# Attention and a mixture of experts on one core: the batches of the attention stage written out, two orders changed

## The chip, the core and the metric

The kernel runs on one core of a Trainium2 chip. The core has a matrix engine (TensorE, PE in the profile, with its weight loads as PEld), three engines for element-wise work (VectorE DVE, ScalarE ACT, GpSimd POOL) and a queue engine that issues most transfers (SyncE, SP). Each engine takes its own list of instructions in order; engines meet at semaphores. The metric is the device time of one execution in microseconds. Before the change it is 4362.92 us (median of 3 runs, 4358.69 to 4367.35).

## The reference

One transformer block in float32 over x of shape 8 x 1024 x 512. Cut to what matters:

```
q, k, v = heads(x @ Wq.T + bq), heads(x @ Wk.T + bk), heads(x @ Wv.T + bv)   # 16 heads of 32
q_lr, k_lr = q @ Wq_lsr, k @ Wk_lsr                                            # per head, rank 32
attn = softmax(causal(q_lr @ k_lr.T / sqrt(32)))
x = layernorm(x + (attn @ v) @ Wo.T + bo)
# experts: 16 of them, each takes the 512 tokens with the largest logit for it
xn = x / rms(x) * norm_weight;  logits = xn @ router.T + bias
y_e = gelu(xn[idx_e] @ fc1_e.T + b1) @ fc2_e.T + b2,   weighted by softmax(logits), summed per token
x = layernorm(x + weighted sum / sum of weights)
```

## The kernel before, in words

The program runs five stages one after the other: folding the weights, attention, selection of tokens, experts, last normalisation. The diff touches the attention stage, `build_attention`, and the lists that order it.

Attention goes batch by batch, eight batches (NB = 8) of 1024 tokens. Per batch there are four slots, one for each group of four heads (`plan_slot`), and then an output phase (`plan_tail`). The lists that these functions return hold items such as ("scores", g, k, h) or ("out", t), and every engine walks through the same list and does its part of each item. So the list sets the order on TensorE, ScalarE, VectorE and GpSimd together. SyncE has its own order, written out in its `run`.

In a slot TensorE makes scores of key blocks (L682), ScalarE takes exponentials into `probs` (L796), GpSimd masks the diagonal blocks (L541), and TensorE multiplies probabilities with values and with ones (L701). Between these stand, for the groups to come, projections of q and k (L670, "proj") and products whose row maxima VectorE takes (L637, L640, L845). Before the next group's operands can be used, SyncE copies strips of q and k into them (`strips`, L435 and L436: 24 transfers) and loads the next weights (L422).

The output phase has eight token tiles, t = 0 to 7. "out" is the product with Wo (L670 from `y_cols`); behind it come, on the other engines, the residual added on VectorE (L878), the statistics (L880), two square roots on ScalarE (L766, L768), and the two normalised forms x1 and xn (L887, L896), both stored by SyncE (L478, L480). "turn" transposes xn on TensorE (L656), ScalarE copies the result into xnT (L772). "logit" is the product with the router for four tiles (L664), copied by L777 and stored by L473. "v" is the value product of the next batch (L670 from `wv_parts`), copied by ScalarE (L728). "invert" is the reciprocal of softmax sums (L869), which belongs to the last group. All products of out, v, turn and logit go through a ring of three banks, `shared_banks`, in the order of the list; a bank is free when its reader is done: for "out" that is the statistics instruction L880.

The residual of tile 0 is loaded before the last group's strips are issued, that of tile 1 after them (L441, in `run` of SyncE).

`probs` has four buffers. x1 is buffer 0, xn buffer 1, xnT buffers 2 and 3. `slot_of(k, pair)` says which buffer the exponentials of key block k use. At the first exponential of a batch ScalarE waits until all stores of x1 and xn are done (L787 to L791).

`each_batch` runs the first seven batches as a loop on the engines, with the batch number in a register, and writes the last batch out behind it. The last batch leaves out the work for a batch to come: no "v" items, and fewer projections and maxima. `lead` is the work before the first batch.

Of the kernel before, what the change touches and what calls it, by code (L numbers as in the profile page):

```python
# [21 lines left out]
GROUPS = HEADS // HG  # L22
T = 1024
TT = T // P
# [7 lines left out]
QT = HALF // P  # L32
# [154 lines left out]
PROB_BUFS = 4  # L187
DEN_PIECES = 4
TURN_LAG = 2
# [43 lines left out]
def plan_tail():  # L233

    order = []
    for t in range(TT + TURN_LAG):
        if t < TT:
            order.append(("out", t))
            if t == 0:
                order += [("invert", GROUPS - 1, 1, i) for i in range(2)]  # L240
            order.append(("v", t))
            if t == 0:
                order += [("invert", GROUPS - 1, 1, i) for i in range(2, DEN_PIECES)]
        if t >= TURN_LAG:
            order.append(("turn", t - TURN_LAG))
            if (t - TURN_LAG) % QT == QT - 1:
                order.append(("logit", (t - TURN_LAG) // QT))
    return order


def plan_lead():
# [23 lines left out]
def build_attention(nc, w, x_dram, xT_dram, x1_dram, table, logits_dram, scratch, keep, NB):  # L275
    with ExitStack() as ctx:
# [11 lines left out]
        v = sb("v_rows", [P, TT, D])  # L288
# [60 lines left out]

        def slot_of(k, pair):  # L350

            return (2 * k + pair) % PROB_BUFS

        assert PROB_BUFS == 4 and (2 * NE) % PROB_BUFS == 0

# [24 lines left out]
        def scope(b, lead=False):  # L380

            if lead:
                return lead_in, lead_turns, [0] * RING
            off = [lead_used[k] + b * batch_used[k] for k in range(RING)]
            if isinstance(b, int) and b == NB - 1:
                return last, last_turns, off
            return batch, batch_turns, off

        def seen_by(b, item, lead=False):

            if lead:
                return lead_seen[item]
            return (last_seen if isinstance(b, int) and b == NB - 1 else batch_seen)[item]

        def await_parts(eng, passed, b, g, lead=False):

# [4 lines left out]

        def each_batch(eng, run):

            if NB > 1:
                with eng.Fori(0, NB - 1) as b:
                    run(b)
            run(NB - 1)

        block = ctx.enter_context(nc.Block())

# [1 line left out]
        def _(sp):  # L412
# [28 lines left out]
                sp.dma_start(xres[:, t % 2], x_dram[bass.ds(b * T + t * P, P), :]).then_inc(res_in[t % 2], 16)  # L441

            def run(b):
                more = not (isinstance(b, int) and b == NB - 1)
                for slot in range(GROUPS - AHEAD):
                    strips(b, slot)
                    if more or slot + 1 < GROUPS - AHEAD:
                        load_w((slot + AHEAD + 1) % GROUPS)
                if more:
                    load_x(b + 1, b * GROUPS + GROUPS)  # L450
                    strips(b, GROUPS - 2)
                    load_w(1)
                load_residual(b, 0)
                if more:
                    strips(b, GROUPS - 1)
                    load_w(2)
                for t in range(1, TT + TURN_LAG):

                    if t < TT:
                        load_residual(b, t)  # L460
                    if t >= TURN_LAG:
                        store(b, t - TURN_LAG)
                        if t - TURN_LAG == QT:
                            store_logits(b, 0)
                store_logits(b, 1)
# [36 lines left out]
        def _(pool):  # L502
# [48 lines left out]

            def run(b):
                order, _, _ = scope(b)
                more = not (isinstance(b, int) and b == NB - 1)
                for item in order:
                    if item[0] == "invert" and item[3] == DEN_PIECES - 1:
                        normalise(b, item[1], item[2])
# [155 lines left out]
        def _(act):  # L713
# [70 lines left out]
            def exps(b, g, k, h):  # L784
                c0 = steps[k][2]
                s = (b * GROUPS + g) * NE + k
                act.wait_ge(st_full, HG * s + h + 1)  # L787
                if g == 0 and k == 0 and h == 0:

                    for r in range(2):  # L790
                        act.wait_ge(x1_out[r], 16 * (TT // 2) * b)  # L791
                        act.wait_ge(xn_out[r], 16 * (TT // 2) * b)
# [898 lines left out]
```

## Time and profile before

| what | value |
|---|---|
| median of 3 runs | 4362.92 us |
| the profiled execution: time, span | 4363.62 us, 4361.9 us |
| mean granted TensorE clock | 0.914 |
| TensorE busy | 3794.3 us, 87% of the span |
| VectorE, ScalarE, GpSimd busy | 52%, 34%, 16% |

A row of the timeline gives start and length in us, engine, source line, operation, output and input tiles, shapes and how often; a bracket at its end is the time that the engine was idle before, and what released it ("issue": nothing that the profile shows). Starts count from the beginning of the span. Attention ends at about 2570 us of it, experts take most of the rest. The granted clock is given as a share of 2.4 GHz: 1.00, or 0.50 for 1.2 GHz.

### The profile page before, as it was taken

The page shows a single profiled execution, that of the slowest core. Times are in us where ns is not written, and L with a number is a line of the kernel's source. Part 1 is how long each engine was busy: PE and PEld are TensorE (multiplying, and loading weights), DVE is VectorE, ACT ScalarE, POOL GpSimd, SP SyncE. Part 2 cuts the span into 40 slices and gives each one's busy share as a digit, 9 for nine tenths or more (in the row PEclk, how much of TensorE's full clock was granted, in tenths as well). Part 3 has the DMA queues.
Part 4 walks back from the last instruction along what each step waited for, and adds up shares of the span by engine and source line. Part 5 has one row for each costly group of instructions (what it writes and reads, how often), then busy time and mean ns, then how long its engine had stood idle before and what let it go on. Part 6 is the DMA issues. An engine that isn't in the chain of part 4 may idle for free. (4 is left out here: it accounts for less than half of the span.)

```text
span 4361.9 us, 64361 instructions
## 1 busy us (share of the span) xinstructions
PE 3794.3 (87%) x21481; PEld 2590.9 (59%) x21481; DVE 2257.6 (52%) x3990; ACT 1471.7 (34%) x2754; POOL 686.1 (16%) x859
## 2 busy tenths in 40 slices
PE   5898999998998998989989951799999999999990
PEld 3555555555555555555555420788888888888880
DVE  3565555554664654655655547544444444444444
ACT  1342432442442433433434410333333333333324
POOL 2121121121121121211211110011111111021100
PEclk8899999998999999999999975599999999999995
DMA  4224233133133322331342120233334433344328
GB/s 151 63 77 117 58 86 105 46 100 96 42 98 96 80 75 82 98 91 55 91 113 64 35 64 0 88 119 119 118 104 128 128 119 119 114 122 124 119 68 317
DMA packets 187436, 424.18 MB, mean 97 GB/s; under 512 B 39776, under 2 KB 42848, under 8 KB 178400
## 3 DMA queue, kind: packets, MB, share of 16 engines
q1 hardware_dynamic: 167408, 367.98, 28.0%
q0 software_dynamic: 14336, 34.09, 4.3%
q10 hardware_dynamic: 5376, 17.83, 1.0%
q8 instruction: 207, 3.39, 0.3%
q14 instruction: 109, 0.89, 0.1%
HBM read 245.70 MB, written 72.38 MB: 73 GB/s over the span
## 5 line engine op out<-in xcount | busy, mean ns | idle before, releaser
L845 DVE TENSOR_REDUCE max_slots<-shared_banks 128x1 f32<-128x512 f32 (+3 forms) x1536 | 790.0, 550 | 501.4 <-PE shared_banks L640 378.7
L796 ACT ACTIVATE probs<-scores_t 128x512 f32<-128x512 f32 (+3 forms) x1536 | 677.8, 494 | 789.7 <-PE scores_t L682 733.9
L1514 PE MATMUL m_ps_h<-m_tokens_t,m_w_parts 128*128 128x512 f32 x3072 | 743.4, 391 | 15.2 <-issue 13.6
L1514 PE MATMUL m_ps_y<-m_w_parts,m_hidden_parts 128*128 128x512 f32 x3072 | 736.5, 389 | 0.3
L1514 PEld LDWEIGHTS m_ps_h<-m_tokens_t,m_w_parts 128*128 128x128 f32 x3072 | 575.1, 188 | 138.5 <-issue 20.6
L1514 PEld LDWEIGHTS m_ps_y<-m_w_parts,m_hidden_parts 128*128 128x128 f32 x3072 | 575.9, 188 | 123.1 <-issue 3.7
L637 PE MATMUL shared_banks<-k_operands,q_operands 96*128 96x512 f32 (+3 forms) x1536 | 540.1, 403 | 89.6 <-DMA k_operands<-natural 79.1
L682 PE MATMUL scores_t<-q_operands,k_operands 128*128 128x512 f32 (+3 forms) x1536 | 543.3, 404 | 51.0 <-ACT probs L796 22.6
L637 PEld LDWEIGHTS shared_banks<-k_operands,q_operands 96*128 96x128 f32 x1536 | 314.0, 207 | 273.1 <-issue 134.2
L1421 ACT ACTIVATE m_hidden<-m_ps_h,m_b 128x512 f32<-128x512 f32 x256 | 176.6, 690 | 834.2 <-PE m_ps_h L1514 821.0
L541 POOL TENSOR_SCALAR_AFFINE_SELECT probs<-probs 128x256 f32<-128x256 f32 x512 | 208.3, 408 | 1431.3 <-ACT probs L796 1431.1
L1479 DVE CAST m_hidden_parts<-m_hidden 128x512 fp32r<-128x512 f32 x256 | 110.7, 432 | 599.2 <-ACT m_hidden L1421 599.0
L670 PE MATMUL shared_banks<-x_parts,wqk_group 128*128 128x512 f32 x1536 | 385.4, 403 | 32.9 <-DVE x_parts L901 18.3
L682 PEld LDWEIGHTS scores_t<-q_operands,k_operands 128*128 128x128 f32 x1536 | 287.4, 203 | 188.1 <-issue 109.0
L701 PE MATMUL y_bank<-probs,v_rows 128*32 128x512 f32 (+3 forms) x3072 | 348.8, 528 | 1.5 <-POOL probs L541 1.5
L670 PEld LDWEIGHTS shared_banks<-x_parts,wqk_group 128*128 128x128 f32 x1536 | 289.9, 194 | 96.7 <-issue 19.1
L701 PE MATMUL den_bank<-probs,ones_f 128*32 128x512 f32 (+3 forms) x3072 | 326.8, 498 | 0.0
L1379 POOL DMA_INDIRECT scratch_x<-m_out,m_idx x64 | 114.0, 1781 | 1160.6 <-DVE m_out L1498 1146.0
L670 PE MATMUL shared_banks<-wv_parts,x_parts 128*128 128x512 f32 x768 | 227.9, 450 | 67.4 <-DVE ln_stats L880 67.1
L640 PE MATMUL shared_banks<-mask_q_rows,ident_bf 128*128 128x128 bf16 x1024 | 246.2, 243 | 0.0
L670 PE MATMUL shared_banks<-wo_cols,y_cols 128*128 128x512 f32 x512 | 236.1, 605 | 4.2 <-DVE ln_stats L880 4.2
L670 PEld LDWEIGHTS shared_banks<-wv_parts,x_parts 128*128 128x128 f32 x768 | 156.4, 205 | 130.9 <-DVE ln_stats L880 72.8
(202 smaller groups left out, 3205.3 us busy)
## 6 DMA issues: line engine op xcount, KB each, us to landing
m_w_raw<-in_w1T SPq DMA_DIRECT2D x64, 1024.0 KB, 5.1
m_w_raw<-in_w2T SPq DMA_DIRECT2D x64, 1024.0 KB, 7.4
q_operands<-natural SPq DMA_DIRECT2D x384, 128.0 KB, 2.5
k_operands<-natural SPq DMA_DIRECT2D x384, 128.0 KB, 2.5
wqk_group<-scratch_wqk SPq DMA_DIRECT2D x32, 1024.0 KB, 5.2
natural<-in_xT SPq DMA_DIRECT2D x8, 2048.0 KB, 8.7
x_residual<-in_x SPq DMA_DIRECT2D x64, 256.0 KB, 2.8
scratch_x<-probs SPq DMA_DIRECT2D x64, 256.0 KB, 2.1
```

The lines of the kernel that those rows point to most:

```text
L541: pool.affine_select(out=block, in_=block, compare_op=ALU.is_ge, fill=0.0, base=0, pattern=[[0, 2], [1, P]], channel_multiplier=-1).then_i ...
L637: mm = pe.matmul(out[:, 0:n], q_ops[0:MAX_STRIP, buf, h, it * P:(it + 1) * P], k_ops[0:MAX_STRIP, buf, h, k0:k0 + n], start=True, stop=not ...
L640: mm = pe.matmul(out[:, n - P:n], identb[:], mask_q[:], start=False, stop=True)
L670: mm = pe.matmul(out, a, c, start=(n == 0), stop=(n == len(pairs) - 1))
L682: pe.matmul(st[:, (HG * k + h) % SCORE_BANKS, c0:HALF], k_ops[:, buf, h, j * P:(j + 1) * P], q_ops[:, buf, h, hh * HALF + c0:(hh + 1) * HA ...
L701: mm = pe.matmul(bank[h * DH:(h + 1) * DH, c0:HALF], rows(h, j), probs[:, slot_of(k, h // 2), h % 2, c0:HALF], start=(j == 0), stop=(j == ...
L796: act.activation(probs[:, slot_of(k, h // 2), h % 2, c0:HALF], st[:, (HG * k + h) % SCORE_BANKS, c0:HALF], ACT.Exp, scale=SCALE).then_inc( ...
L845: dve.tensor_reduce(mx[:, h, slot:slot + 1], src[:, 0:n], AX.X, ALU.max).then_inc(bank_free[bank], 1)
L1379: pool.indirect_dma_start(out=x1_dram[:, :], out_offset=bass.IndirectOffsetOnAxis(ap=idx[:, r, j:j + 1], axis=0), in_=out[:, j, :], in_off ...
L1421: act.activation(h[:, f % 2, :], ps_h[:, f % 2, 0:CAP], ACT.Gelu, bias=b1[:, r, f:f + 1]).then_inc(gelu_done, 1)
L1479: dve.tensor_copy(hs[:, f % 2, HI, :], h[:, f % 2, :]).then_inc(h_hi, 1)
L1514: mm = pe.matmul(bank, a, b, start=(first and n == 0), stop=(final and n == len(pairs) - 1))
```

## The change

Three things. `each_batch` writes all eight batches out, so no engine has a loop or a batch number in a register here. `slot_of` is shifted by two buffers: the first key block of a batch uses buffers 2 and 3, and ScalarE's wait for the stores of x1 and xn moves from the first key block to the second (and is dropped for the first batch). `plan_tail` orders a tile as out, turn of two tiles before, values of the tile before; all four reciprocals follow the first out; the last turns, the last values and the second logits come at the end. The other lines take away a test that only a loop needs.

```diff
--- before.py
+++ after.py
@@ -233,19 +233,17 @@
 def plan_tail():
 
     order = []
-    for t in range(TT + TURN_LAG):
-        if t < TT:
-            order.append(("out", t))
-            if t == 0:
-                order += [("invert", GROUPS - 1, 1, i) for i in range(2)]
-            order.append(("v", t))
-            if t == 0:
-                order += [("invert", GROUPS - 1, 1, i) for i in range(2, DEN_PIECES)]
+    for t in range(TT):
+        order.append(("out", t))
+        if t == 0:
+            order += [("invert", GROUPS - 1, 1, i) for i in range(DEN_PIECES)]
         if t >= TURN_LAG:
             order.append(("turn", t - TURN_LAG))
-            if (t - TURN_LAG) % QT == QT - 1:
-                order.append(("logit", (t - TURN_LAG) // QT))
-    return order
+        if t >= 1:
+            order.append(("v", t - 1))
+        if t == TURN_LAG + QT - 1:
+            order.append(("logit", 0))
+    return order + [("turn", TT - 2), ("turn", TT - 1), ("v", TT - 1), ("logit", 1)]
 
 
 def plan_lead():
@@ -349,7 +347,7 @@
 
         def slot_of(k, pair):
 
-            return (2 * k + pair) % PROB_BUFS
+            return (2 * k + pair + 2) % PROB_BUFS
 
         assert PROB_BUFS == 4 and (2 * NE) % PROB_BUFS == 0
 
@@ -382,7 +380,7 @@
             if lead:
                 return lead_in, lead_turns, [0] * RING
             off = [lead_used[k] + b * batch_used[k] for k in range(RING)]
-            if isinstance(b, int) and b == NB - 1:
+            if b == NB - 1:
                 return last, last_turns, off
             return batch, batch_turns, off
 
@@ -390,7 +388,7 @@
 
             if lead:
                 return lead_seen[item]
-            return (last_seen if isinstance(b, int) and b == NB - 1 else batch_seen)[item]
+            return (last_seen if b == NB - 1 else batch_seen)[item]
 
         def await_parts(eng, passed, b, g, lead=False):
 
@@ -401,10 +399,8 @@
 
         def each_batch(eng, run):
 
-            if NB > 1:
-                with eng.Fori(0, NB - 1) as b:
-                    run(b)
-            run(NB - 1)
+            for b in range(NB):
+                run(b)
 
         block = ctx.enter_context(nc.Block())
 
@@ -441,7 +437,7 @@
                 sp.dma_start(xres[:, t % 2], x_dram[bass.ds(b * T + t * P, P), :]).then_inc(res_in[t % 2], 16)
 
             def run(b):
-                more = not (isinstance(b, int) and b == NB - 1)
+                more = not (b == NB - 1)
                 for slot in range(GROUPS - AHEAD):
                     strips(b, slot)
                     if more or slot + 1 < GROUPS - AHEAD:
@@ -551,7 +547,7 @@
 
             def run(b):
                 order, _, _ = scope(b)
-                more = not (isinstance(b, int) and b == NB - 1)
+                more = not (b == NB - 1)
                 for item in order:
                     if item[0] == "invert" and item[3] == DEN_PIECES - 1:
                         normalise(b, item[1], item[2])
@@ -785,7 +781,7 @@
                 c0 = steps[k][2]
                 s = (b * GROUPS + g) * NE + k
                 act.wait_ge(st_full, HG * s + h + 1)
-                if g == 0 and k == 0 and h == 0:
+                if g == 0 and k == 1 and h == 0 and b > 0:
 
                     for r in range(2):
                         act.wait_ge(x1_out[r], 16 * (TT // 2) * b)
```

In TensorE's list the output phase begins, before the change, with three outs (`wo_cols`) and three value products (`wv_parts`) in turn, and the first transpose (`ident_f,probs`) behind them:

```order
L670 MATMUL shared_banks<-wo_cols,y_cols 128x512 x4
L670 MATMUL shared_banks<-wv_parts,x_parts 128x512 x12
L584 REGISTER_ALU
L670 MATMUL shared_banks<-wo_cols,y_cols 128x512 x4
L584 REGISTER_ALU
L670 MATMUL shared_banks<-wv_parts,x_parts 128x512 x12
L670 MATMUL shared_banks<-wo_cols,y_cols 128x512 x4
L584 REGISTER_ALU
L670 MATMUL shared_banks<-wv_parts,x_parts 128x512 x12
L584 REGISTER_ALU
L654 ISA
L656 MATMUL shared_banks<-ident_f,probs 128x128 x4
```

After the change the same place reads:

```order
L666 MATMUL shared_banks<-wo_cols,y_cols 128x512 x8
L666 MATMUL shared_banks<-wv_parts,x_parts 128x512 x12
L666 MATMUL shared_banks<-wo_cols,y_cols 128x512 x4
L652 MATMUL shared_banks<-ident_f,probs 128x128 x4
L666 MATMUL shared_banks<-wv_parts,x_parts 128x512 x12
L666 MATMUL shared_banks<-wo_cols,y_cols 128x512 x4
L652 MATMUL shared_banks<-ident_f,probs 128x128 x4
```

The first value product moved behind the second out, the second behind the first transpose. The register and ISA rows are gone.

At the end of the phase TensorE has, before the change, the last two transposes, the logit product (`router_weight`) and the jump, and below it the first scores of the batch written behind the loop:

```order
L656 MATMUL shared_banks<-ident_f,probs 128x128 x4
L584 REGISTER_ALU
L654 REGISTER_ALU
L656 MATMUL shared_banks<-ident_f,probs 128x128 x4
L661 REGISTER_ALU
L664 MATMUL shared_banks<-probs,router_weight 32x128 x16
L405 REGISTER_ALU
L405 COMPARE_AND_BRANCH
L682 MATMUL scores_t<-q_operands,k_operands 128x512 x4
```

After the change:

```order
L666 MATMUL shared_banks<-wv_parts,x_parts 128x512 x12
L652 MATMUL shared_banks<-ident_f,probs 128x128 x8
L666 MATMUL shared_banks<-wv_parts,x_parts 128x512 x12
L660 MATMUL shared_banks<-probs,router_weight 32x128 x16
L678 MATMUL scores_t<-q_operands,k_operands 128x512 x4
```

A value product stands between the last two transposes and the logit product, and the scores follow with no branch.

In ScalarE's list, with the semaphores each row waits for, the step from the loop to the batch behind it reads before the change (L777 copies the logits, L796 are exponentials):

```order
L777 ACTIVATE logits_half<-shared_banks,router_bias 128x128 [waits bank1_full,logits_out1]
L405 REGISTER_ALU
L405 COMPARE_AND_BRANCH
L796 ACT_TABLE_LOAD [waits x1_out1,xn_out1,xn_out0,pv_done,x1_out0]
L796 ACTIVATE probs<-scores_t 128x512 [waits st_full] x4
L796 ACTIVATE probs<-scores_t 128x384 [waits pv_done,st_full]
```

After the change, between any two batches:

```order
L773 ACTIVATE logits_half<-shared_banks,router_bias 128x128 [waits bank1_full,logits_out1]
L792 ACT_TABLE_LOAD [waits pv_done]
L792 ACTIVATE probs<-scores_t 128x512 [waits st_full] x4
L792 ACTIVATE probs<-scores_t 128x384 [waits x1_out1,xn_out1,xn_out0,pv_done,x1_out0,st_full]
L792 ACTIVATE probs<-scores_t 128x384 [waits st_full] x3
```

The waits for x1_out and xn_out went from the table load to the second key block's first exponential.

## Rows read from the trace of the kernel before

**Rows 1.** Page, part 1: busy time of each engine (share of the span) and instructions.
```profile
PE 3794.3 (87%) x21481; PEld 2590.9 (59%) x21481; DVE 2257.6 (52%) x3990; ACT 1471.7 (34%) x2754; POOL 686.1 (16%) x859
```

**Rows 2.** Timeline of TensorE, first output phase: start, us, engine, line, out<-in, [idle <-releaser].
```profile
410.55 5.49 PE L670 MATMUL shared_banks<-wv_parts,x_parts 128*128 128x512 f32 x12 [10.30 <-DVE ln_stats L880]
415.83 0.71 PE L656 MATMUL shared_banks<-ident_f,probs 128*128 128x128 f32 x4
416.38 3.60 PE L670 MATMUL shared_banks<-wo_cols,y_cols 128*128 128x512 f32 x8
419.41 3.37 PE L670 MATMUL shared_banks<-wv_parts,x_parts 128*128 128x512 f32 x12
422.62 0.60 PE L656 MATMUL shared_banks<-ident_f,probs 128*128 128x128 f32 x4
```

**Rows 3.** Timeline of the other engines and queues around the gap ended at 410.55.
```profile
384.47 0.52 SPq L435 DMA_DIRECT2D q_operands<-natural  x1
...
401.39 0.94 SPq L441 DMA_DIRECT2D x_residual<-in_x  x2
...
407.78 2.48 POOL L567 TENSOR_TENSOR x_residual<-x_residual,bo_folded 128x512 f32<-128x512 f32 x2 [11.09 <-DMA x_residual<-in_x]
409.07 0.69 DVE L878 TENSOR_TENSOR probs<-shared_banks,x_residual 128x512 f32<-128x512 f32 x1 [13.76 <-POOL x_residual L567]
...
411.25 0.57 ACT L728 ACTIVATE v_rows<-shared_banks 128x512 f32<-128x512 f32 x1
```

**Rows 4.** List of waits, whole span: who waited for whom, us, times, longest us.
```profile
PE shared_banks L670 <- DVE ln_stats L880: 71.2, 8, 10.3
...
PE scores_t L682 <- issue: 21.6, 6, 3.8
```

**Rows 5.** Timeline of TensorE, both logit products and the first step between batches.
```profile
437.31 1.08 PE L664 MATMUL shared_banks<-probs,router_weight 128*32 128x128 f32 x32 [0.74 <-ACT probs L772]
...
454.30 1.08 PE L664 MATMUL shared_banks<-probs,router_weight 128*32 128x128 f32 x32 [0.69 <-ACT probs L772]
459.12 1.64 PE L682 MATMUL scores_t<-q_operands,k_operands 128*128 128x512 f32 x3 [3.74 <-issue]
462.11 1.67 PE L682 MATMUL scores_t<-q_operands,k_operands 128*128 128x512 f32 x3 [1.35 <-ACT probs L796]
```

**Rows 6.** Timeline of all engines at the seventh step, out of the loop.
```profile
2315.89 0.98 PE L682 MATMUL scores_t<-q_operands,k_operands 128*128 128x512 f32 x3
2316.08 0.37 ACT L777 ACTIVATE logits_half<-shared_banks,router_bias 128x128 f32<-128x128 f32 x1 [1.26 <-PE shared_banks L664]
...
2318.19 1.28 ACT L796 ACT_TABLE_LOAD   x1 [1.74 <-DMA scratch_table<-probs]
...
2320.13 1.67 PE L682 MATMUL scores_t<-q_operands,k_operands 128*128 128x512 f32 x3 [3.27 <-ACT probs L796]
...
2327.98 0.39 PE L682 MATMUL scores_t<-q_operands,k_operands 128*128 128x256 f32 x1
```

**Rows 7.** Windows: us, then PE, PEld, DVE, ACT, POOL busy (instructions), PEclk, DMA, GB/s.
```profile
460.00:464.00 4.00, 2.65 (x8) 1.50 (x7) 0.00 (x0) 3.83 (x7) 0.71 (x2) 0.50 0.00 0
...
472.00:476.00 4.00, 4.00 (x45) 2.06 (x41) 2.89 (x6) 1.35 (x5) 1.44 (x4) 1.00 0.00 0
```

**Rows 8.** Timeline of TensorE: the same projection after a shorter and a longer pause.
```profile
616.86 4.60 PE L670 MATMUL shared_banks<-x_parts,wqk_group 128*128 128x512 f32 x12 [1.78 <-POOL x_parts L531]
...
1237.52 3.01 PE L670 MATMUL shared_banks<-x_parts,wqk_group 128*128 128x512 f32 x12 [1.28 <-POOL x_parts L531]
```

**Rows 9.** Timeline of TensorE: second wait for strips, in the loop and behind it.
```profile
581.77 0.47 PE L637 MATMUL shared_banks<-k_operands,q_operands 96*128 96x128 f32 x1 [3.27 <-DMA k_operands<-natural]
...
2439.05 0.45 PE L637 MATMUL shared_banks<-k_operands,q_operands 96*128 96x128 f32 x1 [3.29 <-DMA k_operands<-natural]
```

**Rows 10.** Timeline of ScalarE: two table loads of the first batch.
```profile
148.78 1.28 ACT L796 ACT_TABLE_LOAD   x1 [6.02 <-PE scores_t L682]
...
384.84 1.28 ACT L766 ACT_TABLE_LOAD   x1
```

## The prediction

> **What bounds the kernel now.** I read the page first. TensorE is busy 87% of the span, no other engine over 52% [rows 1], so the question is where TensorE stands still or runs slow, and whether the change touches those places. The change touches the attention stage alone (eight batches), and in it only the end of a batch and the step into the next. So I read TensorE's timeline through the output phase of the first batch, then the list of waits, then all engines around the two longest gaps.
>
> The output phase has one long gap. After three out-projections and two value products TensorE waits 10.30 us and resumes at 410.55 with a value product that needs the bank of the second out-projection [rows 2]. The reader should follow that wait back by the releasers: the normalisation of that tile starts at 409.07 after 13.76 us of waiting for GpSimd; GpSimd waited 11.09 us for the residual's DMA; that DMA is issued at 401.39, because SyncE issues the strips of the next group first, from 384.47 on [rows 3]. The same wait stands eight times in the list, 71.2 us in all [rows 4]; seven are the batches with value products, the eighth is the short one of the last batch. From 415.83 on TensorE's rows follow each other without a bracket of idle time, so the rest of the phase is bound by TensorE itself.
>
> The step into the next batch has two gaps. The second logit product starts at 454.30. Then come 3.74 us in which TensorE waits for nothing the profile shows, three score products (1.64 us), and 1.35 us of waiting for the first exponential [rows 5]. "Issue" gaps before the scores stand six times, 21.6 us [rows 4]: the six times that the loop jumps back. The seventh step, from the last turn of the loop to the batch written behind it, has no jump, and there the scores follow the logit product with no idle time [rows 6].
>
> **The change part by part.** All sums are against the profiled execution, which took 4363.62 us (its span 4361.9), 0.7 us above the median of the runs.
>
> *Loop written out.* The seventh step shows the price of a step without a jump. There ScalarE finishes the logits at 2316.45 (2316.08 + 0.37), waits 1.74 us for the stores of the normalised tile, loads its table (1.28 us) and starts the exponentials; TensorE, after three scores in 0.98 us, waits 3.27 us and goes on at 2320.13 [rows 6]. So with the loop gone alone, a step has 3.27 us of idle TensorE time in place of 3.74 + 1.35.
>
> *Probabilities in the other buffers.* The stores that ScalarE waits for read the buffers that the first exponentials used to overwrite. In the new order the wait sits before the second key block, four exponentials later. By then it is over: the normalised tile of the last token block is ready some 3.5 us earlier against the logit product than before, since a value product (3.2 us) now stands between them. The 1.74 us go, and 3.27 becomes 1.53 us. Late next is the table load itself (1.28 us), which must come after the logits are copied.
>
> Together, for six steps: 21.6 + 6 x 1.35 - 6 x 1.53 = 20.5 us, and the three scores no longer run at half clock (1.64 against 0.98 us [rows 5, 6]), 6 x 0.66 = 4.0: **-24.5 us**. The seventh step gives its 1.74: **-1.7 us**. The first batch has a table load at 148.78 [rows 10] that the order after the change does not have; it stands after the scores, so exponentials start 1.28 us earlier, but TensorE then runs at half clock, so I take **-1 us** (0.6 to 1.3).
>
> *The clock behind the step.* TensorE's granted clock is 0.50 (1.2 GHz) in the window 460 to 464 and 1.00 (2.4 GHz) at 472 to 476 [rows 7]. At the seventh step the work from 2320.13 to 2327.98 takes 7.85 us; about 1.6 of it is paced by exponentials, the other 6.2 would be half as long at full clock, so 3.1 us are at stake per step. What will 1.53 us of idleness do? The trace has two neighbours: after 1.28 us a twelve-matmul product took 3.01 us (full clock), after 1.78 us it took 4.60 [rows 8], 1.6 more. The new gap lies between; as paced scores follow it, I go by the nearer worse row: a loss of 1.6 stays, 1.5 is won, seven times: **-10.5 us**. Bounds: 0 (clock falls as long as now) and -21.7 (never falls).
>
> *Order out, turn, values.* This part costs. The gap ends when the residual comes, which no part of the change moves: SyncE's strips and loads stand in the same order. But before the gap TensorE now does out, out, values, out, one value product fewer than before, and a turn is what meets the missing bank. So one value product more, 3.21 us by the pitch of rows [rows 2], stands behind the gap. Also, ScalarE's copy of the first value product now stands behind the square roots of the late tile: it will end about 411.82 as the same copy does now [rows 3], and the next value product needs its bank. Before: value product at 410.55, turn, next out-projection at 416.38. Then: turn at 410.55 (0.7), a wait until 411.85, value product at half clock to 416 and its rest at full clock, out-projection near 416.8: +0.4. At the other end the order pays back: both logit products waited for the copy of the turn just before them, 0.74 and 0.69 us [rows 5]; now a value product hides that copy. Sum per batch: 3.21 + 0.4 - 1.43 = 2.2, times seven: **+15.3 us**. Bounds: +8, if the half-clock stretch ends sooner, to +27, if it lasts one stretch longer (1.6 more each, from rows 8). The last batch has no value products, and its order stays as it was.
>
> In the steady part of the phase I find no new wait: every out-projection uses one bank, every turn the second, every value product the third, and each is copied or measured while the two others run (3.0 and 3.2 us against copies of 0.6).
>
> *Register instructions.* They go from all five queues. What they cost is bounded by the same stretch in and out of the loop: from the fourth score to the batch's second wait for strips it takes 119.66 us in the loop (462.11 to 581.77) and 118.92 outside (2320.13 to 2439.05) [rows 5, 6, 9], which is 0.74 us for two of a batch's four groups, so 0 to 10 us for seven batches. The clock's ups and downs make as much difference, and TensorE's long stretches have no idle time in which such instructions show, so I take **-1 us**.
>
> Sum: -24.5 - 1.7 - 1 - 10.5 + 15.3 - 1 = -23.4. 4363.6 - 23.4 = 4340.2; against the median 4339.5, say **4340 us**.
>
> **A rule that speaks against a term.** The 1.74 us before ScalarE's table load are put down by the trace to a DMA, and the table load after the last y copy of a group, at 384.84, follows the copy at once, without idle time [rows 6, 10]. The Trainium skill, "ScalarE: Activation LUTs", section "What ACT_TABLE_LOAD costs", says that a switch of the table costs, beside the load, a drain of about 1.38 us. The trace of the load itself agrees with its 1.28 us; the drain I do not see at 384.84. By that rule most of the 1.74 would stay, and the time would be that of the first rival, 4363 us.
>
> **Rivals.**
>
> *The idle time before the table load is ScalarE's own.* Then moving the wait gives nothing: all seven steps keep 3.27 us, and the clock falls as it does now. Lost against my sum: 7 x 1.74 + 10.5 = 22.7, so 4363 us, no change. For it: the load follows other work of ScalarE by 1.74 us. Against it: the row names the DMA, and 384.84 shows a load without a pause.
>
> *The clock stays up behind the step.* Then all 21.7 us are won in place of 10.5: 4329 us. For it: the row after 1.28 us at full clock. Against it: 1.78 us was enough to lose it, and after the new gap three scores come at the pace of exponentials, not back to back.
>
> *Values wait for ScalarE at every tile.* This one ends slower. ScalarE takes its work in order; a value copy now stands behind the square roots of the tile one later, and so behind that tile's residual. If residuals land late at each of the tiles behind the gap, TensorE waits at each value product as it will at the first (0.6 us or more). At six products of seven batches 0.6 us is 25 us, no change (4365); at 1.2 us it is 50 us: 4390 us. It decides from about 0.8 us per product on. Against it: from 415.83 on TensorE runs without a gap, so residuals were early there, and the pitch of a tile stays the same.
>
> *The change in the order of code doesn't remove the gap.* Straight code must be brought in too; if it came no faster than after a jump, 3.7 us would stay somewhere in each batch: 4340 + 22 = 4362. Against it: the batch outside the loop is straight code and has no such gap at its start [rows 6].
>
> **How the numbers follow.** Forecast, 4340, with the clock and tail terms between their bounds (4328 to 4354): 0.66. Clock stays up, near 4329: 0.15. ScalarE's own pause: 0.05. Straight code slow: 0.03. Values wait at every tile: 0.11, half of it slower than before. A measurement of this kernel tells 0.2% (8.7 us) from no change. Faster than 4354: 0.66 + 0.15 and a little of the others, 0.84; within: 0.10; slower: 0.06. Range 4324 to 4358.
>
> **What would show it.** Right: no "issue" gap before the scores in any batch; the table load directly behind the logit copy and no wait for the stores; some 1.5 us of idle TensorE time there; in the output phase a turn, not a value product, that ends the long wait, which becomes about 3 us longer (12 to 13.5 us); no gap before the logit products; logit products about 2 us later against the end of the gap. Wrong: the long wait ends at another time against the strips' issue, value products with gaps at each tile, a pause before the table load, or a half-clock stretch behind the step as long as now.

## The result and the profile after

Beside runs of the kernel before on the same chip (median 4360.81 us, 4357.2 to 4367.35), the changed kernel took **4326.84 us** (median of 4 runs, 4321.81 to 4329.64): a ratio of 0.9919 with a 95% interval of 0.9902 to 0.9936. It is faster, by 34 us where 23 were forecast, and inside the range. The sum was nearer than its terms: a term that was not in it (the experts, -15.8 us) stands beside a gain of the clock that was forecast three times too large and a cost of the order that was a third too large. So the total came near in part by luck. The profiled execution after has a span of 4327.9 us against 4361.9 before, 34.0 less.

The first view to read is TensorE's timeline through the first output phase and the step behind it (start, us, engine, line, operation, out<-in, then the idle time before it and what ended it). Lines of the kernel are four less than before.

```profile
379.92 7.13 PE L666 MATMUL shared_banks<-wo_cols,y_cols 128*128 128x512 f32 x16
...
405.38 1.11 PE L652 MATMUL shared_banks<-ident_f,probs 128*128 128x128 f32 x4 [12.09 <-DVE ln_stats L876]
406.71 5.30 PE L666 MATMUL shared_banks<-wv_parts,x_parts 128*128 128x512 f32 x12 [0.22 <-ACT v_rows L724]
411.85 3.59 PE L666 MATMUL shared_banks<-wo_cols,y_cols 128*128 128x512 f32 x8
415.28 0.60 PE L652 MATMUL shared_banks<-ident_f,probs 128*128 128x128 f32 x4
415.63 3.04 PE L666 MATMUL shared_banks<-wv_parts,x_parts 128*128 128x512 f32 x12
...
431.96 1.08 PE L660 MATMUL shared_banks<-probs,router_weight 128*32 128x128 f32 x32
...
447.92 3.05 PE L666 MATMUL shared_banks<-wv_parts,x_parts 128*128 128x512 f32 x12
450.90 1.08 PE L660 MATMUL shared_banks<-probs,router_weight 128*32 128x128 f32 x32
451.91 0.96 PE L678 MATMUL scores_t<-q_operands,k_operands 128*128 128x512 f32 x3
454.43 1.42 PE L678 MATMUL scores_t<-q_operands,k_operands 128*128 128x512 f32 x3 [1.57 <-ACT probs L792]
...
460.87 0.39 PE L678 MATMUL scores_t<-q_operands,k_operands 128*128 128x256 f32 x1
```

Against [rows 2, 5] the reader is to see four things. A turn now ends the long wait, which is 12.09 instead of 10.30 us. One value product (5.30 us, at a granted clock of 0.50 to 0.54) stands behind it. Neither logit product waits any more (the two waits that are left in the list, 6.4 us, are those of the last batch, which has no value products). And in the step 1.57 us of idle time are left of 3.74 + 1.35. The list of waits says the same of all batches (who waited for whom, us in all, times, longest); there is no issue wait before the scores in it:

```profile
PE shared_banks L652 <- DVE ln_stats L876: 85.6, 7, 13.2
...
PE scores_t L678 <- ACT probs L792: 20.6, 39, 1.6
```

ScalarE's table load follows the copy of the logits at once, at this step as at the seventh, where [rows 6] had 1.74 us between them:

```profile
2296.26 0.37 ACT L773 ACTIVATE logits_half<-shared_banks,router_bias 128x128 f32<-128x128 f32 x1 [0.51 <-PE shared_banks L660]
2296.65 1.28 ACT L792 ACT_TABLE_LOAD   x1
```

What was not foreseen lies in code that the change does not touch. The experts' group in part 5 of the page (busy us, mean ns | idle us before, by what ended it), first before, then after:

```profile
L1514 PE MATMUL m_ps_h<-m_tokens_t,m_w_parts 128*128 128x512 f32 x3072 | 743.4, 391 | 15.2 <-issue 13.6
```

```profile
L1510 PE MATMUL m_ps_h<-m_tokens_t,m_w_parts 128*128 128x512 f32 x3072 | 740.4, 391 | 1.6 <-DVE m_tokens_t L1448 1.6
```

Where the 34.0 us went, each part summed from the same start times in both profiled executions over all places where it stands:

| Stretch | before | after | moved | forecast |
|---|---|---|---|---|
| start to first out-projection of batch 0 | 384.09 | 379.92 | -4.2 | -1 |
| output phases, first out-projection to second logit product, x7 | 484.0 | 495.5 | +11.5 | +15.3 |
| steps, logit product to fourth score, loop's six | 45.7 | 21.2 | -24.4 | -24.5 |
| the seventh step | 5.26 | 3.54 | -1.7 | -1.7 |
| behind the step, fourth score to third key block, x7 | 55.8 | 52.7 | -3.1 | -10.5 |
| rest of the batches, to the next out-projection, x7 | 1543.7 | 1544.2 | +0.4 | -1 |
| the last batch's output phase, to the first product of the selection | 65.3 | 68.7 | +3.4 | 0 |
| experts, first expert product to the last | 1442.0 | 1426.2 | -15.8 | 0 |

The parts add up to -33.9. The stretches that the forecast had priced come to -21.5 against its -23.4; the last two, -12.4 together, stood in its sum at nothing.

### The profile page after: what moved, and what is told of

Its sections match the earlier page's. It is cut to its first block and busy times, and to the rows that moved or that the text cites. A ratio compares the mean times of both kernels' runs of the same rounds, so it can differ in the third digit from the quotient of the medians.

```text
span 4327.9 us, 57451 instructions
## 1 busy us (share of the span) xinstructions
PE 3784.8 (87%) x21481; PEld 2587.7 (60%) x21481; DVE 2268.5 (52%) x3990; ACT 1469.1 (34%) x2753; POOL 685.9 (16%) x859
## 5 line engine op out<-in xcount | busy, mean ns | idle before, releaser
L841 DVE TENSOR_REDUCE max_slots<-shared_banks 128x1 f32<-128x512 f32 (+3 forms) x1536 | 790.5, 551 | 484.2 <-PE shared_banks L636 365.1
L666 PE MATMUL shared_banks<-x_parts,wqk_group 128*128 128x512 f32 x1536 | 386.2, 404 | 35.2 <-DVE x_parts L897 18.5
L865 DVE RECIPROCAL denominators<-denominators 128x128 f32<-128x128 f32 x256 | 227.6, 924 | 0.9
L666 PE MATMUL shared_banks<-wv_parts,x_parts 128*128 128x512 f32 x768 | 213.3, 430 | 1.8 <-ACT v_rows L724 1.5
```

Of the source, the lines that this page charges most:

```text
L666: mm = pe.matmul(out, a, c, start=(n == 0), stop=(n == len(pairs) - 1))
L841: dve.tensor_reduce(mx[:, h, slot:slot + 1], src[:, 0:n], AX.X, ALU.max).then_inc(bank_free[bank], 1)
L865: dve.reciprocal(den[:, cols], den[:, cols]).then_inc(rden_ready, 1)
```

## The experiments

**The experts: where their code lies.** The code of the experts' loop is some 1670 instructions of TensorE a turn. In the changed kernel it begins at another place, since the batches ahead of it are written out. The queue that fetches instructions (packets, MB, share) moved less, first before, then after:

```profile
q8 instruction: 207, 3.39, 0.3%
```

```profile
q8 instruction: 126, 2.06, 0.2%
```

That is 16.4 KB a packet. 55 of the 81 packets less are those of the experts. Between 2990 and 4050 us, from the second turn of their loop to the seventh, the kernel before moves

```profile
q8 instruction: 53, 0.87, 0.3%
```

and the changed kernel, over the same turns, none. The first two kernels move the code and nothing else; 128 increments of a semaphore that nobody reads stand ahead of the experts:

```
+            for _ in range(128):
+                pe.sem_inc(padding, 1)
             pe.wait_ge(consts, 1)
```

On the changed kernel: 

> The changed kernel with 128 semaphore increments on TensorE's queue just ahead of the experts, so that the code of the experts' loop lies 128 instructions further along; nothing else differs. Theory (the experts became 15.8 us shorter only because the loop's code came to lie across one block of fetched code less): the issue gaps come back at the loop's returns, twelve of 0.6 to 2 us, a pair of experts takes about 181.3 instead of 178.3 us, and the kernel about 4340 to 4344 us beside 4327 for the changed kernel; the increments themselves cost under 3 us, once. Rival (the gaps left because the attention's code is straight, or because the experts' inputs come otherwise): no gaps, 4327 to 4330 us.

It took 4332.11 us (4327.68 to 4339.85), 5.3 over the changed kernel and under the expected 4340 to 4344; the two intervals overlap, so it is the gaps and the packets that tell here, not the time. The gaps are back, twelve of them, but smaller than I expected (7.6 us in all, not 13 to 16).

On the kernel before: 

> The kernel before with the same 128 increments at the same place, its loop over the batches kept. Theory (the code's place): the twelve issue gaps among the experts go, a pair of experts takes about 178.3 instead of 181.3 us, and the kernel 4345 to 4349 us beside 4361 for the kernel before. Rival (the attention's straight code): the gaps stay, 4361 to 4364 us.

It took 4346.33 us against 4361.13, a ratio of 0.9968 (0.9956 to 0.9981), within the expected range. The gaps among the experts are gone, while the loop over the batches and its gaps stay. Two more offsets, one run each:

> The changed kernel with 64 instead of 128 increments ahead of the experts: the loop's code moves by 64 instructions and still lies across seven blocks of 256. Theory (the count of blocks decides): no issue gaps at the loop's returns, a pair of experts 178.3 us, 4327 to 4331 us. Rival (any move of the code from its place brings the gaps): six or more gaps of 0.6 to 2 us, as with 128.

> The same with 220 increments: the loop's code begins near the end of a block and lies across eight blocks. Theory: the issue gaps are there, six to twelve, in all 5 to 16 us; a pair of experts 179.5 to 181.3 us. Rival (gaps only by chance of what else is fetched): none.

Both missed: 64 instructions further on, gaps; 220 further on, none. The waits of the four kernels, in the order 128 on the changed kernel, 64, 220, and 128 on the kernel before:

```profile
PE m_ps_h L1511 <- issue: 7.6, 12, 1.0
```

```profile
PE m_ps_h L1511 <- issue: 4.0, 6, 0.9
...
PE m_ps_h L1511 <- DVE m_tokens_t L1449: 1.6, 1, 1.6
```

```profile
PE m_ps_t L1551 <- issue: 36.3, 1, 36.3
PE m_ps_h L1511 <- DVE m_tokens_t L1449: 1.6, 1, 1.6
```

```profile
PE scores_t L682 <- issue: 22.3, 6, 4.0
...
PE m_ps_h L1515 <- DVE m_tokens_t L1453: 1.7, 1, 1.7
```

The packets of q8 go with the gaps. With the code moved by 128 and by 64 there are 181 of them:

```profile
q8 instruction: 181, 2.97, 0.3%
```

That is 55 more than the 126 of the changed kernel; moved by 220 there are 127, and in the kernel before the move takes 53 away (207 to 154). In the kernels with gaps some nine packets fall into every turn; in those without there is none for six turns (12 or 13 among the experts in all, in the first turn and near the end, against 67). So at a return either the whole loop is fetched again, or nothing of it is. It is thereby shown that the place of the code decides, and with it whether the loop is fetched anew. My rule for which place is bad (eight blocks of 256 instructions against seven, counted from the start of the program) is refuted as I counted it: the starts that fetch nothing are 27, 38 and 247 past a multiple of 256, those that do are 91, 97, 155 and 166. A start measured from another point would put the first three into one stretch and the others outside it; that was not tried. The Trainium skill, "Runtime: NRT & Kernel Launch", section "Instruction fetch mechanics", says that TensorE holds 128 KiB of instructions, refilled in blocks of 16 KiB (256 instructions), and that a jump to code not held must wait for it. The packet's 16.4 KB and the gaps at the returns agree with that; the size held is shown by no run here. (The increments themselves are not free: 36.3 us of issue wait with 220 of them, where 16.4 us of waiting for a DMA stood.)

**The change in parts.** First the loop written out alone, with the old order and the old buffers (`slot_of` gives `(2 * k + pair)` again, the stores are waited for at `k == 0`, `plan_tail` is the old one):

> The changed kernel with the old order of the output phase and with the probabilities in the old pair of buffers: of the change only the written-out batches. Theory: the step between logits and scores loses its issue time (about 3.8 us down to none) but keeps the wait for ScalarE, so that it is about 5.3 us at all seven places instead of 7.7 at six: -14 to -16; first batch about -4, experts -15.8, clock behind the step -3; the output phases as before (69.1 us each). Together about 4324 to 4328 us, close to the changed kernel, since what the other buffers give (7 x 1.74 = 12 us) and what the order takes (11.5 us) are nearly equal. Rival (the other buffers do it, straight code little): steps stay above 7 us and the time above 4335 us.

It took 4312.18 us against 4361.13 (ratio 0.9886, 0.987 to 0.9903): 14.7 us *faster* than the whole change, and under the expected 4324 to 4328. All seven steps take 3.53 us, not 5.3. TensorE and ScalarE there, at the first step:

```profile
452.24 0.96 PE L680 MATMUL scores_t<-q_operands,k_operands 128*128 128x512 f32 x3
454.76 1.42 PE L680 MATMUL scores_t<-q_operands,k_operands 128*128 128x512 f32 x3 [1.55 <-ACT probs L794]
```

```profile
452.43 0.37 ACT L775 ACTIVATE logits_half<-shared_banks,router_bias 128x128 f32<-128x128 f32 x1 [1.34 <-PE shared_banks L662]
452.81 1.28 ACT L794 ACT_TABLE_LOAD   x1
```

The reader is to see that the table load comes at once although ScalarE must wait for the stores here: they had landed. So the 1.74 us of [rows 6] are no property of the old buffers; they go with the loop. In the kernel before, the last store of xn ahead of a step took 3.8 to 5.2 us to land at every one of the seven steps; here it takes 2.0 us at all seven. What was moved from the issue of that store on, at the seventh step before (2313.6 to 2318.1 us), then here (2279.7 to 2281.8 us):

```profile
q8 instruction: 1, 0.02, 1.3%
...
scratch_table<-probs SPq DMA_DIRECT2D x1, 256.0 KB, 4.4
```

```profile
q1 hardware_dynamic: 281, 0.51, 64.9%
...
scratch_table<-probs SPq DMA_DIRECT2D x1, 256.0 KB, 2.0
```

Before, a packet of the instruction queue falls among those of the store; here there is none. The thirteen kernels have 91 such steps. At 68 the store landed in 2.0 to 2.1 us. At the other 23 a packet of 16.4 KB of q8 started 1.0 to 2.0 us behind its issue, and it landed after 2.35 to 5.22 us: these are all 21 steps of the three kernels with the loop, and one each of the copies moved by 128 and by 220. That such a packet holds the store up fits every step; no kernel moved one by itself to show it.

Then with the other buffers as well, so that only the order is missing:

> The changed kernel with the old order of the output phase: written-out batches and the other pair of buffers. Theory (the new order costs 1.65 us in each of seven output phases, since a value product stands behind the long wait): 4314 to 4317 us, output phases 69.1 us from the first output product to the second group of logits, steps 3.5 us; 10 to 12 us under the kernel with written-out batches alone. Rival (the longer output phase of the changed kernel comes from the other buffers or from the straight code, not from the order): phases 70.8 us and 4325 to 4329 us.

4308.30 us (4307.46 to 4314.59; ratio 0.9885, 0.9869 to 0.9902), 18.5 us faster than the whole change, under the expected 4314 to 4317, and not told apart from the loop written out alone (0.9886), from which 10 to 12 us were expected. The steps are the same 3.53 us. The seven output phases are 484.2 us, 11.3 less than with the new order, as expected. Of the 21.9 us between the two spans (4306.0 and 4327.9) another 5.7 lie behind the steps (46.9 against 52.7 in all), 2.2 in the last batch's output phase, and 2.7 in three other stretches. The 5.7 I do not put down to the order: kernels with the same new order ranged from 48.0 to 53.0 there.

The order alone, in the kernel before with its loop and its buffers:

> The kernel before with the new order of the output phase, its loop over the batches and its buffers kept. Theory: the order costs 1.65 us in each of eight or seven phases, and the experts' code stays across the same count of blocks: 4371 to 4376 us beside 4361. Rival (the cost of the order comes only with straight code): 4359 to 4363 us.

4365.86 us against 4360.34 (ratio 1.0013, 1.0003 to 1.0022). The output phases are 495.1 us, 11.2 more; the steps give back 5.1 (45.8 against 50.9), 2.9 of it issue time (18.7 us in the list instead of 21.6) and 1.7 at the seventh, where the store now had landed in time. So the order alone is a loss, smaller than expected (4371 to 4376) by what the steps gave back.

**The clock behind the step.** Five matmuls whose result nothing reads fill TensorE's idle time between the third and the fourth score:

```
+                if b > 0 and g == 0 and k == 0 and h == SCORE_BANKS:
+                    pe.wait_ge(y_drained, 2 * b * GROUPS)
+                    for _ in range(5):
+                        pe.matmul(yb[:, 0:HALF], k_ops[:, buf, 0, 0:P], q_ops[:, buf, 0, 0:HALF], start=True, stop=True)
                 pe.wait_ge(exp_done, s + 1)
```

> The changed kernel with five matmuls whose result nothing reads, on TensorE between the third and the fourth score of each of the seven steps, where it otherwise stands for about 1.6 us behind ScalarE's first exponentials. Theory (it is this idle time that lets the granted clock fall behind the step): the clock stays at 1.00 behind all seven steps, the stretch from the fourth score to the first score of the third step takes 4.9 us at each instead of 6.4 to 8.1, and the kernel is about 18 us shorter than the changed kernel: 4306 to 4311 us. Rival (the clock falls because of what stands ahead of the step, or by the light load of the scores themselves): the stretches keep 6.4 to 8.1 us, 4325 to 4330 us, or a little more for the matmuls added.

4311.76 us (4306.53 to 4318.02; ratio 0.9881, 0.9866 to 0.9896), 15.1 under the changed kernel. Windows from the fourth score to the third key block (us, then PE, PEld, DVE, ACT, POOL busy, granted clock as a share of 2.4 GHz, DMA, GB/s), four of the seven steps of the changed kernel:

```profile
454.40:460.90 6.50, 6.42 (x31) 2.83 (x31) 2.66 (x5) 3.19 (x7) 1.62 (x4) 0.74 0.02 4
...
1065.90:1074.00 8.10, 8.05 (x31) 3.25 (x31) 2.66 (x5) 3.17 (x7) 1.62 (x4) 0.58 0.01 1
1372.90:1381.00 8.10, 8.03 (x31) 3.19 (x31) 2.66 (x5) 3.19 (x7) 1.62 (x4) 0.58 0.01 1
...
2298.60:2306.50 7.90, 7.90 (x31) 3.34 (x31) 2.66 (x5) 3.17 (x7) 1.62 (x4) 0.57 0.01 3
```

and with the idle time filled:

```profile
457.00:461.90 4.90, 4.84 (x31) 2.16 (x31) 2.37 (x5) 3.17 (x7) 1.63 (x4) 1.00 0.02 5
...
1066.90:1071.80 4.90, 4.83 (x30) 2.14 (x31) 2.37 (x5) 3.18 (x7) 1.63 (x4) 1.00 0.01 2
1370.80:1375.70 4.90, 4.83 (x30) 2.14 (x31) 2.37 (x5) 3.18 (x7) 1.64 (x4) 1.00 0.01 2
...
2288.20:2293.10 4.90, 4.82 (x30) 2.14 (x30) 2.37 (x5) 3.19 (x7) 1.64 (x4) 1.00 0.02 5
```

The same work, the same seven exponentials beside it, and 4.9 us at 1.00 in all seven instead of 6.4 to 8.1 us at 0.56 to 0.74. The added matmuls cost nothing, since TensorE still waits after them:

```profile
455.27 1.31 PE L680 MATMUL y_bank<-q_operands,k_operands 128*128 128x512 f32 x5
457.01 1.42 PE L682 MATMUL scores_t<-q_operands,k_operands 128*128 128x512 f32 x3 [0.42 <-ACT probs L796]
```

So it was the 1.57 us of idle time, and not what stands ahead of it or the pace of the scores, that cost the clock: 52.7 - 34.2 = 18.5 us in all. The time fell by 3.4 us less than that; in this kernel six gaps among the experts came back (3.9 us), its code having moved by 70 instructions, to 97.

**The long wait itself.** SyncE loads the residual of tiles 1 to 4 ahead of or between the strips, no longer behind all four sets (the residual of tile 2 is issued at 383.09 in the second kernel below; after the change at 396.92, with that of tile 1, behind all the strips):

```
-                if more:
-                    strips(b, GROUPS - 1)
-                    load_w(2)
...
+                    if more and t <= HG:
+                        strips(b, GROUPS - 1, heads=(t - 1,))
+                    if more and t == HG:
+                        load_w(2)
```

With the new order of the output phase: 

> The changed kernel with another order on SyncE's queue in the output phase: the residual rows of tiles 1 to 4 go ahead of or between the four transfers of the last group's strips, instead of behind all four. Theory (the long wait of about 12 us at tile 1 is a wait for residual rows that queue behind the strips): the wait goes, seven times, so some -75 to -84 us: about 4243 to 4252 us. Rival (the wait is VectorE's own lateness or the strips are needed as early): the wait becomes 5 us or more at this or at the next tile and the gain is under 40 us.

4246.87 us against 4360.34 (ratio 0.9753, 0.9733 to 0.9772): 80 us under the changed kernel, as expected. With the old order:

> The same order on SyncE's queue, with the old order of the output phase on TensorE. Theory (the new order costs only because it puts a value product behind the long wait, and its later turns and logits save about 1.4 us a batch): with the wait gone the old order is the slower one, by 4 to 12 us against the kernel with the new order and the same queue. Rival (the new order is the longer one whatever stands before tile 1): the old order is 8 to 14 us faster here as well.

4226.37 us (ratio 0.9701, 0.9685 to 0.9717): my theory on the order fell; the old order is *20.5 us faster* here. The seven output phases are 414.6 us with the new order and 406.5 with the old. The rows where the turn stands, new order first:

```profile
388.19 3.59 PE L668 MATMUL shared_banks<-wo_cols,y_cols 128*128 128x512 f32 x8
393.56 0.66 PE L654 MATMUL shared_banks<-ident_f,probs 128*128 128x128 f32 x4 [1.78 <-DVE ln_stats L878]
394.89 3.06 PE L668 MATMUL shared_banks<-wv_parts,x_parts 128*128 128x512 f32 x12 [0.68 <-ACT v_rows L726]
```

```profile
690.80 0.60 PE L656 MATMUL shared_banks<-ident_f,probs 128*128 128x128 f32 x4
691.24 3.60 PE L670 MATMUL shared_banks<-wo_cols,y_cols 128*128 128x512 f32 x8
694.27 3.37 PE L670 MATMUL shared_banks<-wv_parts,x_parts 128*128 128x512 f32 x12
697.48 0.60 PE L656 MATMUL shared_banks<-ident_f,probs 128*128 128x128 f32 x4
```

With the turn ahead of the value product, the wait for the bank of an earlier tile (1.8 us) and for the value copy behind ScalarE's square roots (0.68 us) stand open at TensorE; in the old order a value product covers both (in some batches a wait of less than 1 us stays at the next out-projection, and the logit products wait as before). TensorE's idle time in the seven phases is 22.7 us with the new order and 19.4 with the old, its mean granted clock there 0.992 and 1.000. The order costs apart from the long wait. Behind the steps the two differ by another 8.0 us (48.3 against 40.3), which is the clock again and not shown to be the order's.

**Both together**, the old order, the residuals between the strips, and the five matmuls:

> The fastest kernel so far (written-out batches, the other buffers, the old order of the output phase, the residual rows between the strips) with the five added matmuls in each step. Theory: its stretches behind the step, 4.9 to 7.9 us and 40.3 us in all, become 7 x 4.9 = 34.2: 4218 to 4222 us beside 4226. Rival: no gain, 4225 to 4229 us.

4220.39 us against 4360.92 (ratio 0.9672, 0.9658 to 0.9685), the fastest kernel here, 106 us under the changed one. All seven stretches behind the step take 4.88 us. Its lead over the kernel without the matmuls (0.9701) is not told apart for certain, since the two intervals meet at 0.9685, and 3.9 us of gaps among the experts came back with them.

## Why the prediction was right, and where it was not

*The step, forecast -24.5 and -1.7, measured -24.4 and -1.7.* Size right, half the reason wrong. "So with the loop gone alone, a step has 3.27 us of idle TensorE time" is the sentence that failed: with the loop alone gone it has 1.55 us at all seven steps. I took the seventh step, which has no jump back, for a step without the loop, and its wait for the stores for a property of the buffers. It has the loop's late store (4.4 us, and a wait of 1.74; in the moved copy of the kernel before 4.5 and 1.89), with a packet of the instruction queue among the store's own; written out, the store lands in 2.0 us. That the sum came out right is luck: the term for the loop and the term for the buffers were added, and the loop, written out, did all of it. The other buffers gave nothing that these runs can tell.

*ScalarE's own pause before its table load.* Not seen: no load in any step waits in a kernel with the batches written out, with either buffers; it follows the copy within 0.02 us. The drain of the rule that I weighed is not seen there.

*The clock, forecast -10.5, measured -3.1.* The mis-sized term, and the largest miss inside the sum. I knew that the gap of 1.57 us lay between a pause that kept the clock and one that lost it [rows 8], and went by the worse of the two, a loss of 1.6 us a step. What the runs showed: a loss of 2.6 us a step in the mean (52.7 - 34.2, by seven). The stretch takes about 4.9, 6.4 or 8.0 us, and at this gap it took the longer two at all seven steps of the changed kernel. The rival "the clock stays up" was wrong for the change, yet its price was right: with the gap filled the seven stretches take 34.2 us against 55.8 before, 21.6 less where that rival said 21.7.

*The order, forecast +15.3, measured +11.5.* Right in kind. Per batch, from the end of the long wait to the second logit product it takes 45.19 instead of 43.40 us, 1.8 against my 2.2. The value product behind the gap, the wait for ScalarE's copy (0.22 us) and the vanished waits of the logit products are all there in the rows. The forecast that the long wait grows by 3 us came out at 2.6 (85.6 / 7 = 12.2 us against 9.6). What I did not see is that the order would cost without the long wait too.

*Values wait for ScalarE at every tile.* Wrong, for the reason given: after 411.85 value products follow the turns without a gap, and the one short wait for ScalarE's copy stands seven times in the list, once a batch.

*Register instructions, forecast -1, measured +0.4 over the rest of the batches.* They cost nothing that shows.

*The first batch, forecast -1, measured -4.2.* The term was too small. The table load is gone as said: from the first score to the fifth it takes 2.07 instead of 3.59 us, 1.5 less where I allowed 1.3 at most. From the first score to the first out-projection the ten kernels with written-out batches take 232.9 to 234.4 us and the three with the loop 236.0 to 237.1, so some 3 us go with the change; what makes the half of them that is not the table load stays open. Of the 4.2 us, 1.4 lie ahead of the first score, which both kinds of kernel reach anywhere from 145.0 to 147.8 us: scatter of the start.

*Left out: the experts, -15.8, and the last output phase, +3.4.* I priced the change where it edits and not where its code pushes other code. That the 15.8 us go with the place of the loop is shown; which places are bad is open. The 3.4 us go with VectorE: its multiply takes 1.8 instead of 0.75 us when GpSimd's add on the residual begins just before it, and after the change the two met so at three tiles running, before at one.

```profile
2517.84 1.27 POOL L563 TENSOR_TENSOR x_residual<-x_residual,bo_folded 128x512 f32<-128x512 f32 x1 [2.01 <-DMA x_residual<-in_x]
2517.88 1.78 DVE L892 SCALAR_TENSOR_TENSOR probs<-probs,rms_inverse,norm_weight 128x512 f32<-128x512 f32 x1
```

The Trainium skill, "SBUF — State Buffer", section "SBUF: two separate sides", says that VectorE with two inputs from SBUF and GpSimd lock a shared port against each other for a whole instruction; the 1.05 us lost here is near the 1.27 us of GpSimd's instruction, and agrees. In the thirteen kernels all 88 multiplies that took 1.4 to 1.9 us met an add that had begun before them or at most 0.047 us behind; where it began later (271 times), the multiply kept its 0.75 us and the add took 1.4 to 1.84 us. The last output phase took 63.3 to 64.0 us without such a meeting, 65.3 to 66.4 with one, 66.5 to 67.1 with two and 68.5 to 68.7 with three, under either order. So the 3.4 us are not the order's. This was read from the rows and not tried.

## What to carry to other kernels

A gap on TensorE is worth its own length and what the clock loses behind it: 1.57 us of idle time cost up to 3.2 us more here, and useless matmuls in the gap won that back. Judge a reordering by what it places behind a long wait and by what it no longer covers; here one part of the change gained, one gave nothing that shows and one lost, and only kernels with single parts told them apart. A place that is to show a kernel without its loop must be free of everything that the loop brings, a late transfer too. When written-out code or a longer program moves a loop, look at that loop's issue gaps and at the packets of the instruction queue, before and after.

## What the runs showed of the hardware

- The returns of a loop of some 1670 instructions cost 0, 3.9 to 4.0, 7.6, 13.6 or 15.8 us in all, by where its code began; the instruction queue moved 53 to 55 packets of 16.4 KB more whenever they cost anything.
- Behind a gap of 1.57 us the stretch of the changed kernel's steps took 1.6 or 3.2 us more than at full clock, at a granted clock between TensorE's two levels (1.2 and 2.4 GHz) in the mean; in two of its three moved copies, at the same gap, sometimes nothing more; with the gap filled down to 0.42 us it was zero at all fourteen steps of two kernels.
- The last store of 256 KB ahead of a step landed in 2.0 to 2.1 us at 68 of 91 steps; at the other 23, each with a packet of 16.4 KB of the instruction queue starting 1.0 to 2.0 us behind its issue, in 2.35 to 5.22 us.
- VectorE's multiply with two inputs from SBUF took 1.4 to 1.9 instead of 0.75 us behind an add of GpSimd, and the add 1.4 to 1.84 instead of 1.27 us behind the multiply.
